# Four neighbouring nodes on each partition in place of two, in a graph attention layer

## The reference

```python
h = jnp.maximum(_layernorm(x, axis=-1), 0.0)
Wh = h @ W
e = (Wh @ a1)[:, None] + (Wh @ a2)[None, :]
e = jax.nn.leaky_relu(e, negative_slope=ALPHA)
scores = jnp.where(adj > 0, e, jnp.float32(NEG_INF))
attention = jax.nn.softmax(scores, axis=1)
x = x + jax.nn.elu(attention @ Wh)
```

## Time and profile before

| | before |
|---|---|
| median of the runs | 697.96 us (697.52 to 698.79) |
| time of the profiled execution | 697.99 us |
| its span | 696.2 us |
| mean granted PE clock | 0.984 |
| PE, ACT, DVE busy | 632.4, 631.3, 620.6 us |
| moved by DMA | 275.13 MB, mean 395 GB/s |

### The profile page before, as it was taken

One profiled execution on the slowest core, in us unless ns is written; L12 is line 12 of the kernel. 1 busy time (PEld: TensorE's weight loads), 2 busy tenths in 40 slices (PEclk: granted clock), 3 DMA queues, 4 the chain that ended last, 5 costly groups with the idle time before them and its releaser, 6 DMA issues.

```text
span 696.2 us, 23856 instructions
## 1 busy us (share of the span) xinstructions
PE 632.4 (91%) x10422; PEld 621.6 (89%) x10422; DVE 620.6 (89%) x625; ACT 631.3 (91%) x366; POOL 54.2 (8%) x51
## 2 busy tenths in 40 slices
PE   4867999999998989989898989989898998989893
PEld 4747999999998989989898989989898998989893
DVE  5898989999989898998989899898989899898982
ACT  5797999999999989989898999989898998989870
POOL 5000001011100101010010101010010101001020
PEclk9987999999999999999999999999999999999997
DMA  9876899999999999999999999999999999999950
GB/s 321 362 302 257 345 373 389 424 427 424 430 425 425 428 427 429 425 425 425 430 425 428 424 428 429 425 426 428 428 423 431 428 425 428 425 427 427 425 216 9
DMA packets 24839, 275.13 MB, mean 395 GB/s; under 512 B 3088, under 2 KB 7440, under 8 KB 8432
## 3 DMA queue, kind: packets, MB, share of 16 engines
q1 hardware_dynamic: 22864, 270.67, 92.8%
q0 software_dynamic: 1488, 4.07, 1.5%
q10 hardware_dynamic: 464, 0.07, 0.1%
HBM read 272.70 MB, written 2.10 MB: 395 GB/s over the span
## 4 chain that ended last, share of the span: by engine, by line
DVE 29%; DMA 29%; ACT 21%; issue 11%; PE 8%; DVEq 1%; ACTq 1%; SPq 0%
DMA adj_ring<-in_adj 28%; DVE code L494 18%; ACT work L357 16%; DVE work L507 4%; ACT work L365 4%; PE psum L738 2%; PE psum L736 2%; PE psum L718 1%; DVE code L501 1%; PE psum L669 1%; DMA Wx<-in_L_gnn_W 1%; PE psum L659 1%; DVE last_steps L525 1%; DVE last_steps L529 1%; ACT trow L340 1%
## 5 line engine op out<-in xcount | busy, mean ns | idle before, releaser
L738 PE MATMUL psum<-V,work 128*128 128x130 f16 x4096 | 495.4, 221 | 0.0
L736 PE MATMUL psum<-V,work 128*128 128x130 f16 x4096 | 495.1, 220 | 0.0
L357 ACT ACTIVATE work<-trow,Wh 128x4096 int8<-128x4096 f32 x128 | 476.7, 3724 | 0.0
L736 PEld LDWEIGHTS psum<-V,work 128*128 128x128 fp8e4 x4096 | 403.2, 98 | 0.0
L738 PEld LDWEIGHTS psum<-V,work 128*128 128x128 fp8e4 x4096 | 398.6, 97 | 0.0
L494 DVE TENSOR_SCALAR code<-adj_ring 128x4096 uint8<-128x4096 int32 x128 | 293.2, 2290 | 31.1 <-DMA adj_ring<-in_adj 31.1
L718 PE MATMUL psum<-identb,code 128*128 128x128 bf16 x2048 | 137.0, 220 | 40.8 <-DVE code L501 40.7
L501 DVE SCALAR_TENSOR_TENSOR code<-work,code 128x1024 int32<-128x1024 int32 x128 | 156.8, 1225 | 7.9 <-ACT work L357 4.0
L718 PEld LDWEIGHTS psum<-identb,code 128*128 128x128 bf16 x2048 | 119.8, 98 | 46.9 <-DVE code L501 30.8
L365 ACT COPY work<-psum 128x1024 int32<-128x1024 int32 x128 | 129.7, 1013 | 34.8 <-PE psum L718 34.8
L507 DVE TENSOR_SCALAR work<-work 128x1024 int32<-128x1024 int32 x128 | 87.9, 686 | 2.3 <-ACT work L365 2.3
(11 more groups left out here) (76 smaller groups left out, 151.2 us busy)
## 6 DMA issues: line engine op xcount, KB each, us to landing
adj_ring<-in_adj SPq DMA_DIRECT2D x128, 2048.0 KB, 16.9
work<-in_x SPq DMA_DIRECT2D x4, 512.0 KB, 6.0
last_steps<-in_x POOLq DMA_DIRECT2D x16, 128.0 KB, 6.6
out_y<-last_steps POOLq DMA_DIRECT2D x15, 128.0 KB, 7.9
out_y<-last_steps SPq DMA_DIRECT2D x1, 128.0 KB, 1.8
W<-in_L_gnn_W ACTq DMA_DIRECT2D x2, 16.0 KB, 5.3
Wx<-in_L_gnn_W ACTq DMA_DIRECT2D x2, 16.0 KB, 5.5
a_sb<-in_L_gnn_a ACTq DMA_DIRECT2D x1, 0.5 KB, 4.0
```

Source lines behind the costliest of these rows:

```text
L357: nc.scalar.activation(sign[:, k % 2].bitcast(I8), trow[:, h * UW:(h + 1) * UW], ACT.Sign, bias=(Wh[:, B, 0:1] if isinstance(B, int) else ...
L736: nc.tensor.matmul(sums_of[:, 0:FP], up8[:, j // 2, j % 2], V[:, jb, 0:FP], start=h == 0 and j == 0, stop=False, skip_group_check=True)
L738: last = nc.tensor.matmul(sums_of[:, FP:2 * FP], down8[:, j // 2, j % 2], V[:, jb, FP:2 * FP], start=False, stop=h == 1 and j == HB - 1, s ...
```

## The change

A partition now holds four neighbouring nodes (`KE` = 4) in place of two.

- Loads of `x` and stores of `out` move 1 KB pieces instead of 512 B pieces: 128 rows of pieces by 4 in L231 (before 128 by 8), 128 pieces in L291, L298 and L260 (before 256).
- A tile of `adj` has the same 128 rows of 16 KB, but the rows of neighbouring partitions lie 128 KB apart in place of 64 KB.
- `spread` writes `trow` at a step of four words in place of two.
- The transposes of the codes read their stationary operand at a step of two bf16 elements (4 bytes) in place of one, to bring the pair (0, 1) or (2, 3) of each group of four columns.
- The `general` block follows the same layout; it is jumped over as before, though it has more instructions.

```diff
-        adj_v = adj.rearrange("(i k p b) j -> k b i p j", p=P, b=2, k=KE // 2)
-        x_i = x.rearrange("(i w p b) f -> i p w b f", p=P, b=2, w=2)
-        out_i = out.rearrange("(i w p b) f -> i p w b f", p=P, b=2, w=2)
+        adj_v = adj.rearrange("(i p b) j -> b i p j", p=P, b=KE)
+        x_i = x.rearrange("(i p b) f -> i p b f", p=P, b=KE)
+        out_i = out.rearrange("(i p b) f -> i p b f", p=P, b=KE)
...
-                xs = x.rearrange("(g p b) f -> p g b f", p=P, b=2)
+                xs = x.rearrange("(g p b) f -> p g b f", p=P, b=KE)
...
-                        sp.dma_start(xh[:, out_of(r), :].rearrange("p (g b) f -> p g b f", b=2),
-                                     xs[:, r * PR:(r + 1) * PR]).then_inc(s_x[r], 16)
+                        sp.dma_start(xh[:, out_of(r), :].rearrange("p (g b) f -> p g b f", b=KE),
+                                     xs[:, r * RR // KE:(r + 1) * RR // KE]).then_inc(s_x[r], 16)
...
-                    rows = adj_v[b // 2, b % 2]
+                    rows = adj_v[b]
...
-                sp.dma_start(out_i[NI - 1], res[:, :, :].rearrange("p (w b) f -> p w b f", b=2)).then_inc(s_last, 16)
+                sp.dma_start(out_i[NI - 1], res).then_inc(s_last, 16)
...
-                    pool.dma_start(xg[:, :, :].rearrange("p (w b) f -> p w b f", b=2), x_i[i]).then_inc(s_xg, 16)
+                    pool.dma_start(xg, x_i[i]).then_inc(s_xg, 16)
...
-                    pool.dma_start(out_i[i], res[:, :, :].rearrange("p (w b) f -> p w b f", b=2)).then_inc(s_out, 16)
+                    pool.dma_start(out_i[i], res).then_inc(s_out, 16)
...
-                    nc.scalar.activation(trow[:, r * TR * P:(r + 1) * TR * P].rearrange("p (g q b) -> p g b q", q=P, b=2),
-                                         t_ps[r].rearrange("p (g b q) -> p g b q", q=P, b=2), ACT.Copy)\
+                    nc.scalar.activation(trow[:, r * TR * P:(r + 1) * TR * P].rearrange("p (g q b) -> p g b q", q=P, b=KE),
+                                         t_ps[r].rearrange("p (g b q) -> p g b q", q=P, b=KE), ACT.Copy)\
...
-                    mine = code[:, k % RM].bitcast(BF16)
+                    mine = code[:, k % RM].bitcast(BF16).rearrange("p (g q e) -> p g e q", q=P, e=2)
...
-                        last = nc.tensor.transpose(into[:, g * P:(g + 1) * P], mine[:, g * P:(g + 1) * P], identb[:, :])
+                        last = nc.tensor.transpose(into[:, g * P:(g + 1) * P], mine[:, g // 2, g % 2], identb[:, :])
```

More of the change, by code:

```diff
@@ L227, in _ @@
             def _(sp):
-                xs = x.rearrange("(g p b) f -> p g b f", p=P, b=2)
-                with nc.allow_non_contiguous_dma(reason="pairs of rows of x, 512 bytes each"):
+                xs = x.rearrange("(g p b) f -> p g b f", p=P, b=KE)
+                with nc.allow_non_contiguous_dma(reason="four rows of x, 1 KB each"):
                     for r in range(NR):
-                        sp.dma_start(xh[:, out_of(r), :].rearrange("p (g b) f -> p g b f", b=2),
-                                     xs[:, r * PR:(r + 1) * PR]).then_inc(s_x[r], 16)
+                        sp.dma_start(xh[:, out_of(r), :].rearrange("p (g b) f -> p g b f", b=KE),
+                                     xs[:, r * RR // KE:(r + 1) * RR // KE]).then_inc(s_x[r], 16)
                 def load(i, k, c):
@@ L790, in rows @@
             return what[bass.ds(w, 1), b].rearrange("o p j -> p (o j)")
-        adj_b = adj.rearrange("(w p b) j -> w b p j", p=P, b=2)
-        x_b = x.rearrange("(w p b) f -> w b p f", p=P, b=2)
-        out_b = out.rearrange("(w p b) f -> w b p f", p=P, b=2)
+        adj_b = adj.rearrange("(w p b) j -> w b p j", p=P, b=KE)
+        x_b = x.rearrange("(w p b) f -> w b p f", p=P, b=KE)
+        out_b = out.rearrange("(w p b) f -> w b p f", p=P, b=KE)
         with nc.Block() as general:
@@ L801, in _ @@
                     sp.sem_inc(g_out, ONE)
-                    with sp.Fori(0, NW) as w:
-                        for b in range(2):
-                            sp.wait_ge(g_read, ONE + w * 2 + b)
+                    with sp.Fori(0, NI) as w:
+                        for b in range(KE):
+                            sp.wait_ge(g_read, ONE + w * KE + b)
                             sp.dma_start(A, rows(adj_b, w, b)).then_inc(g_adj, 16)
-                            sp.wait_ge(g_res, ONE + w * 2 + b)
+                            sp.wait_ge(g_res, ONE + w * KE + b)
                             sp.dma_start(xt, rows(x_b, w, b)).then_inc(g_x, 16)
@@ L811, in _ @@
                 with act.If(needed(act)):
-                    with act.Fori(0, NW) as w:
-                        for b in range(2):
-                            i = w * 2 + b
+                    with act.Fori(0, NI) as w:
+                        for b in range(KE):
+                            i = w * KE + b
                             act.wait_ge(g_dve, i * DSTEPS + 6)
@@ L835, in _ @@
                     nc.vector.tensor_copy(Wh1, Wh[:, :, 3:FW]).then_inc(g_Wh1, 1)
-                    with dve.Fori(0, NW) as w:
-                        for b in range(2):
-                            i = w * 2 + b
+                    with dve.Fori(0, NI) as w:
+                        for b in range(KE):
+                            i = w * KE + b
                             def after(k):
@@ L883, in _ @@
                     pe.wait_ge(g_Wh1, 1)
-                    with pe.Fori(0, NW) as w:
-                        for b in range(2):
-                            i = w * 2 + b
+                    with pe.Fori(0, NI) as w:
+                        for b in range(KE):
+                            i = w * KE + b
                             pe.wait_ge(g_res, ONE + i)
@@ L896, in _ @@
                                     jb = r * RR + j
-                                    c = jb // 2 * 2 * P + jb % 2
+                                    c = jb // KE * KE * P + jb % KE
                                     last = nc.tensor.transpose(half[r % 2][:, j * P:(j + 1) * P],
-                                                               score[:, c:c + 2 * P - 1:2], ident[:, :])
+                                                               score[:, c:c + KE * (P - 1) + 1:KE], ident[:, :])
                                 last.then_inc(g_round, 1)
```

## The result

The changed kernel takes 704.69 us (median of 4 runs, 703.64 to 706.40) beside 698.38 us for the kernel before (now of four runs): ratio 1.009, 95% interval 1.0067 to 1.0113. The forecast was no change, 697.5 us; the time lies just above the range's end of 704.5. The profiled execution took 704.14 us, its span is 702.4 us. One slow execution, of 1292.77 us in the run that splits PE's wait for W, left no trace to explain it and is not in any figure here.

The account below looks back on a forecast made before the run. The prediction took engines to set the pace from 28 to about 120 us, then the DMA; from 697.99 us, -0.4 (x and out) and -0.05 (last store) gave 697.5 us, range 696.6 to 699.0, 8 in 10 from 695.3 to 704.5.

Parts of the forecast that it names:

- What bounds the kernel: Whole run: prologue to about 28 us, engines set the pace to about 120 us, then the DMA at 427 GB/s.
- Spreads (L340): Eight spreads in ACT's row of the chain: the step of four words costs 0; bounds nothing to +8.6 us.
- Rival B: Spreads at L340, before 50 us, slow by the 16-byte line: +0.5 to +8.6 us, 702 us at half; chance 0.10.
- W: Loads of W heading the chain in the prologue: taken as 0, between 1.2 us earlier and 0.6 us later.
- x and out of the bodies: Loads of x and stores of out in the DMA-paced part: -0.4 us, bounds 0 and -0.9 us.
- Tiles of adj and transposes: Loads of adj at 128 KB between partitions: 0. Transposes (L718) reading at 4 bytes a column: 0.
- A: Transposes become float32-like, 117 instead of 55 ns a step, PE takes over from the DMA: about 778 us; chance 0.08.
- C: The DMA slows on adj tiles at 128 KB between partitions: +5 us, 703 us, or more; chance 0.09.
- D: W comes sooner in the prologue: -1.2 us, 696.3 us; chance 0.18, with x and out gain at its bound.

## Why the prediction was wrong, step by step

- *What bounds the kernel.* Right: the DMA's rate after 120 us, one for one before. The losses of the prologue did pass to the end: +7.5 us at the marker, +6.33 at the last `edges`, and 1.1 us between them are the shorter bodies.
- *Spreads (L340).* This is the step that failed. Its term in the sum was 0, and the runs put 5.7 us there. The upper bound was one more such time for each spread, 1.08 us, and +0.956 us is what happened. I chose 0 "nearest to L340 itself", though no row had one hit in a line of 16 bytes, and L340 stood at the edge of the rule. The rule of the Trainium skill that I set beside it ("SBUF — State Buffer", section "Door 1: The DMA port swizzle") was right in kind: the traces have 1082 ns with two hits a line and 2038 with one, beside 1016 side by side. It also told rightly that the transposes, with four hits a line, would not slow (98 and 99 ns). A rule against the change and no row on the other side of its threshold deserved more than 0.10.
- *Rival B* gave 702 us as priced at its middle and 706 at its end; the spreads alone came out at +5.7 us, between the two. Not all of their 7.6 us reached the end, and part of what did may be the clock.
- *W.* This term failed too. I put it at 0, with +0.6 us as the worst. It is +2.3 to +4.2 us at PE's start and +2.2 us at the end. I had named the mechanism (pieces of adj that come sooner), but priced it as a single piece, and gave a chance to W coming sooner only. A transfer that heads the chain and shares the engines with the one that is changed needs bounds as wide on the late side.
- *x and out of the bodies.* Right in sign, too small: 0.08 us a body, not 0.03. The term was worked out from queue 0's share of 1.5%, and that row does not see the pieces: it has 1488 packets and 1.5% before and after. Only the period showed the gain.
- *Tiles of adj and transposes.* Both 0, and both measured 0 (ratio 1.0000; 98 and 99 ns). Rivals A and C fall; so does D. The slowing that the Trainium skill tells of at larger pitches ("DMA: Bandwidth & Descriptors", section "Latency and other measured facts") did not show at 128 KB: the rate stayed at 427 GB/s.
- The parts sum: 5.7 + 2.2 - 0.6 (the bodies, ratio 0.9991) + 0 = 7.3 us against the measured 6.3, within the intervals.

## What to carry to other kernels

When a layout change halves the pieces of a transfer, follow the strides into every on-chip copy that restores the order: one write of 4 bytes per 16 bytes of SBUF took ACT 2038 ns in place of 1082, and with the stride on the PSUM side it was 1016. Look at what small loads share the queues with a bulk load that gets shorter, and give the first instruction a wait for just its own data. Where the DMA sets the pace, only bytes and pieces in that stretch pay; here 1.1 us, against 7.5 us lost in the prologue.

## What the runs showed that I had not expected

ACT writes 1024 float32 a partition in 1016 ns side by side, 1082 ns at a step of two words and 2038 ns at a step of four; reading PSUM at a step of 128 words costs nothing. Four loads of W of 16 KB each took 5.1 to 5.6 us to land beside 512 B pieces of x, and the last of them up to 9.9 us beside 1 KB pieces and the loads of adj behind them.

Where the spreads wrote at a step of four, the granted clock from 20 to 80 us fell from 0.89 to 0.86.
